# Blockwise seven-product query projection, values in DRAM, and attention run three half groups later, in a float32 attention and FFN kernel

## The reference

```
h   = einsum('bct,bcd->bdt', x, cond_weights[itok])      # mixes the 32 positions of a sequence
q, k, v = h @ wq, h @ wk, h @ wv                         # 32 query heads, 8 key/value heads, head size 128
q, k = rope(q), rope(k)
att = softmax(causal(q k^T / sqrt(128)));  o = att @ v   # one k and v per group of 4 query heads
x   = x + o @ wo                                         # 4096 -> 512
y   = einsum('bct,bcd->bdt', x, cond2_weights[itok])
x   = x + quantized(fp8(y) @ fp8(w).T + bias)            # largest value of y, and of the product, sets a scale
```

## Time and profile before

| what | us |
|---|---|
| median of 3 runs | 549.95 (549.31 to 550.25) |
| the profiled execution | 550.04 |
| its span on the core | 548.2 |
| PE busy in it | 523.0 |
| DVE busy | 354.0 |
| POOL busy | 232.0 |
| ACT busy | 212.3 |

### The profile page before, as it was taken

One profiled execution on the slowest core, in us unless ns is written; L12 is line 12 of the kernel. 1 busy time (PEld: TensorE's weight loads), 2 busy tenths in 40 slices (PEclk: granted clock), 3 DMA queues, 4 the chain that ended last, 5 costly groups with the idle time before them and its releaser, 6 DMA issues.

```text
span 548.2 us, 8916 instructions
## 1 busy us (share of the span) xinstructions
PE 523.0 (95%) x3281; PEld 417.1 (76%) x3281; DVE 354.0 (65%) x536; ACT 212.3 (39%) x372; POOL 232.0 (42%) x184
## 2 busy tenths in 40 slices
PE   4999999999999999999999999999999999999990
PEld 1987888888888888888888888888888888887530
DVE  5538255666676667666766676666666756675697
ACT  2514214342534263416341634253516251612524
POOL 3426422642664266426632673267326732610002
PEclk9899999999999999999999999999999999999995
DMA  7540500020012001201020202020202000000004
GB/s 229 194 154 0 173 2 1 1 97 1 11 68 96 0 26 50 96 0 47 29 96 0 74 3 96 0 77 0 96 0 77 5 1 0 2 1 0 2 0 153
DMA packets 18046, 26.81 MB, mean 49 GB/s; under 512 B 1995, under 2 KB 6219, under 8 KB 18028
## 3 DMA queue, kind: packets, MB, share of 16 engines
q1 hardware_dynamic: 18028, 26.57, 14.2%
HBM read 24.47 MB, written 2.10 MB: 48 GB/s over the span
## 4 chain that ended last, share of the span: by engine, by line
PE 92%; DVE 5%; DMA 1%; issue 1%; SPq 0%; ACT 0%; DVEq 0%
PE bank L524 27%; PE bank L525 26%; PE bank L526 26%; PE bank L588 3%; PE bank L575 3%; PE bank L643 1%; PE bank L516 1%; PE bank L709 1%; PE bank L504 1%; PE bank L689 1%; DVE xacc L968 1%; DMA wsc<-in_L_ffn_weight_scale 1%; DVE v_all L963 1%; DVE w L763 1%; PE bank L706 1%
## 5 line engine op out<-in xcount | busy, mean ns | idle before, releaser
L784 DVE TENSOR_TENSOR q_cos<-bank,cst 128x512 f32<-128x512 f32 x80 | 55.3, 691 | 105.1 <-ACT q_swap L394 105.1
L293 POOL TENSOR_TENSOR q_rot<-q_cos,q_swap 128x512 f32<-128x512 f32 x64 | 82.5, 1289 | 89.3 <-DVE q_swap L786 89.3
L524 PE MATMUL bank<-wo_hi,o_hi 128*128 128x512 f32 x256 | 101.6, 397 | 1.3 <-issue 1.3
L524 PE MATMUL bank<-hT_hi,wq_hi 128*128 128x512 f32 x256 | 101.3, 396 | 0.0
L525 PE MATMUL bank<-wo_lo,o_hi 128*128 128x512 f32 x256 | 99.8, 390 | 0.0
L525 PE MATMUL bank<-hT_lo,wq_hi 128*128 128x512 f32 x256 | 99.8, 390 | 0.0
L526 PE MATMUL bank<-wo_hi,o_lo 128*128 128x512 f32 x256 | 99.6, 389 | 0.0
L526 PE MATMUL bank<-hT_hi,wq_lo 128*128 128x512 f32 x256 | 99.6, 389 | 0.0
L393 ACT ACTIVATE q_swap<-bank 64x512 f32<-64x512 f32 x80 | 47.6, 596 | 132.1 <-PE bank L526 132.1
L829 DVE TENSOR_TENSOR xacc<-xacc,bank 128x512 f32<-128x512 f32 x64 | 43.4, 677 | 42.6 <-PE bank L526 42.4
L272 POOL TENSOR_TENSOR wo_lo<-raw_o,wo_hi 128x512 fp32r<-128x512 f32 x32 | 43.7, 1386 | 58.7 <-ACT wo_hi L383 58.7
(11 more groups left out here) (137 smaller groups left out, 728.6 us busy)
## 6 DMA issues: line engine op xcount, KB each, us to landing
raw_q<-in_L_attn_wq SPq DMA_DIRECT2D x8, 1024.0 KB, 5.5
raw_o<-in_L_attn_wo SPq DMA_DIRECT2D x8, 1024.0 KB, 5.3
xacc<-in_x SPq DMA_DIRECT2D x4, 512.0 KB, 8.5
raw_k<-in_L_attn_wk SPq DMA_DIRECT2D x8, 256.0 KB, 2.8
out<-xacc SPq DMA_DIRECT2D x8, 256.0 KB, 2.0
raw_o<-in_L_attn_wv SPq DMA_DIRECT2D x1, 1024.0 KB, 7.3
raw_q<-in_L_attn_wv SPq DMA_DIRECT2D x1, 1024.0 KB, 6.8
q_rot<-in_L_ffn_qweight SPq DMA_DIRECT2D x1, 1024.0 KB
```

Of the source, the lines that this page charges most:

```text
L293: pool.tensor_tensor(dst, q_cos[b][:], q_swap[b][:], ALU.add).then_inc(rope_done, 1)
L524: pe.matmul(dst, l_hi, r_hi, start=(i == 0), stop=False)
L784: dve.tensor_tensor(by_t(q_cos[b][:]), by_t(q_ps[ITEM_BANK[k]][:]), cos_b, ALU.mult).then_inc(rope_cos, 1)
```

## The change

**Query projection.** The four query heads of a group are two pairs. A pair is one 512 by 256 block of wq, and the rows are two halves of 512. Seen as a 2 x 2 by 2 x 2 block product (256 channels by one head, 256 channels by 512 rows), before it is eight block products of 6 matmuls. The change makes it of seven by Strassen and Winograd's scheme: the right sides are blocks of hT or sums of them (t_hi, t_lo, made once in the opening), the left sides are blocks of wq or sums (w_sum, made by POOL with four subtractions or additions of 128x256 for each pair, before the split into seven high and low parts). The products go to banks a, b, c, d, b, c, e; ACT saves the first in SBUF (`keep_first`) and DVE combines them with seven additions (`winograd`), three of them into SBUF and four in place in PSUM, which gives two heads for both halves of the rows.

**Halves.** The sixteen stages become sixteen halves (g, h), h being the pair of heads; each does the pair and the key of row half h. Both units of scores come at the end of half (g, 1). The softmax of unit (g-1, h) runs in half (g, h), and attend and project_out of a unit three halves after its own: (g-2, 1) in half (g, 0) and (g-1, 0) in half (g, 1). The halves before (1, 1) have no attended unit. Four units are left for after the last half, together with the rounding of the FFN weights, which was in the opening before.

**Order of PE in a half:** wait for all five cosines of the half before (and, for h = 0, for both transposes of scores, `s_turned`), attend, seven products, key, project_out 0, 1 and 2, for h = 1 both scores, project_out 3.

**Output weights.** ACT and POOL split wo of group g-1 in half (g, 1), now behind the swap and the rope_add of item 4, which is the key (item 4 in the new order; it was item 0).

**Values** go through four SBUF slots to a DRAM tensor, and 256 KB come back for each unit; POOL's copies of them (L282) go. **Opening:** the condition weights are used in float32 in place of three bfloat16 parts, selection and mixing are interleaved with the first values, the smaller constants load first, and DVE makes t and its low part between the value copies.

The core of the diff (lines that are only "..." stand for what is left out, among it most removed lines):

```diff
-SOFT_STEPS = 8
-ITEM_BANK = [0, 1, 2, 0, 1]
+SOFT_STEPS = 7
+PRODUCTS = 7
+SUMS = 7
+SUM_PRODUCT = (2, 3, 4, 5, 5, 6, 7)
+ITEM_SUM = (3, 5, 6, 7)
...
+        a_ps, b_ps, c_ps, d_ps, e_ps, spare_ps = bank[0:6]
+        product_ps = [a_ps, b_ps, c_ps, d_ps, b_ps, c_ps, e_ps]
+        item_ps = [d_ps, b_ps, c_ps, e_ps, a_ps]
+        k_ps = a_ps
+        o_ps = [c_ps, d_ps, spare_ps, e_ps]
+        o2_ps = [b_ps, c_ps, d_ps, e_ps]
+        s_ps = [spare_ps, a_ps]
+        w_ps = bank[6:8]
...
+        def left_part(h, i):
+            a11, a12 = raw_q[:, h, 0:2, 0:HD], raw_q[:, h, 2:4, 0:HD]
+            a22 = raw_q[:, h, 2:4, HD:2 * HD]
+            return (a11, w_sum[:, 1], w_sum[:, 2], a12, w_sum[:, 0], a22, w_sum[:, 3])[i]
...
+            def load_values(g, r):
+                sp.dma_start(v_st[r][:], v_rows[:, r * TPU:(r + 1) * TPU, bass.ds(g * HD, HD)]).then_inc(dma_vst[r], 16)
...
+                pool.tensor_tensor(w_sum[:, 0], a21, a22, ALU.add).then_inc(w_summed, 1)
+                pool.tensor_tensor(w_sum[:, 2], a11, a21, ALU.subtract).then_inc(w_summed, 1)
+                pool.wait_ge(w_summed, 4 * n + 1)
+                pool.tensor_tensor(w_sum[:, 1], w_sum[:, 0], a11, ALU.subtract).then_inc(w_summed, 1)
+                pool.wait_ge(w_summed, 4 * n + 3)
+                pool.tensor_tensor(w_sum[:, 3], a12, w_sum[:, 1], ALU.subtract).then_inc(w_summed, 1)
...
+            def half(g, h, split_wo=None):
+                follow = (g, 1) if h == 0 else (g + 1, 0)
+                more = not (isinstance(g, int) and g == KV - 1 and h == 1)
+                if more:
+                    sum_weights(*follow)
+                rope_add(g, h, 0)
+                rope_add(g, h, 1)
+                if more:
+                    q_low(*follow, 0)
+                    q_low(*follow, 1)
+                rope_add(g, h, 2)
+                if more:
+                    q_low(*follow, 2)
+                rope_add(g, h, 3)
+                if more:
+                    q_low(*follow, 3)
+                rope_add(g, h, 4)
                 if split_wo is not None:
...
+                    for head in range(REP):
+                        wo_low(split_wo, head, wo_lo)
+                if more:
+                    for i in range(4, PRODUCTS):
+                        q_low(*follow, i)
+                    if h == 1:
+                        k_low(g + 1)
...
+                elif hi is wo7_hi:
+                    act.wait_ge(scores_mm, 2 * KV)
+                else:
+                    act.wait_ge(wo_mm, 2 * TPU * g)
+                for head in range(REP):
+                    act.activation(hi[:, head, :], raw_o[:, head, :], ACT.Copy).then_inc(wo_hi_done, 1)
...
+                if k == 4:
+                    act.wait_ge(key_mm, 2 * g + h + 1)
+                else:
+                    act.wait_ge(sum_done, SUMS * (2 * g + h) + ITEM_SUM[k])
+                if not (isinstance(g, int) and n < 2):
+                    act.wait_ge(rope_done, n - 1)
...
+                swap(g, h, 3)
+                if more:
+                    q_high(*follow, 3)
+                swap(g, h, 4)
+                if split_wo is not None:
+                    wo_high(split_wo, wo_hi)
+                if more:
+                    for i in range(4, PRODUCTS):
+                        q_high(*follow, i)
+                    if h == 1:
+                        k_high(g + 1)
...
+            def product(g, h, i):
+                pe.wait_ge(wq_lo_done, PRODUCTS * (2 * g + h) + i + 1)
+                r_hi, r_lo = right[i]
+                three_pass(product_ps[i][:], [((wq_hi[:, i, c, :], wq_lo[:, i, c, :]), (r_hi[:, c, :], r_lo[:, c, :]))
+                                              for c in range(2)]).then_inc(prod_mm, 1)
+            def pair(g, h, last):
+                n = 2 * g + h
+                if isinstance(g, int) and n == 0:
+                    pe.wait_ge(t_lo_done, 4)
+                else:
+                    pe.wait_ge(rope_cos, 5 * n)
+                    if h == 0:
+                        pe.wait_ge(s_turned, 2 * g)
+                product(g, h, 0)
+                product(g, h, 1)
+                if last is not None:
+                    u = 2 * last[0] + last[1]
+                    pe.wait_ge(o_lo_done, BPT * u + 1)
+                product(g, h, 2)
+                if last is not None:
+                    pe.wait_ge(o_lo_done, BPT * u + 2)
+                product(g, h, 3)
+                pe.wait_ge(sum_done, SUMS * n + 1)
+                product(g, h, 4)
+                pe.wait_ge(sum_done, SUMS * n + 2)
+                product(g, h, 5)
+                if last is not None:
+                    pe.wait_ge(o_lo_done, BPT * u + 4)
+                product(g, h, 6)
+            def key(g, h):
+                pe.wait_ge(wk_lo_done, g + 1)
+                pe.wait_ge(first_kept, 2 * g + h + 1)
+                three_pass(k_ps[:], [((wk_hi[:, c, :], wk_lo[:, c, :]), (hT_hi[:, c, half_rows[h]], hT_lo[:, c, half_rows[h]]))
+                                     for c in range(KC)]).then_inc(key_mm, 1)
...
+            def project_out(g, r, j, left=(o_hi, o_lo), weights=(wo_hi, wo_lo)):
+                n = TPU * (2 * g + r) + j
                 if j == 0:
                     pe.wait_ge(wo_lo_done, REP * (g + 1))
...
+                    pe.wait_ge(o_lo_done, BPT * (2 * g + r + 1))
...
+            def half(g, h, last=None, fill=()):
+                n = 2 * g + h
                 if last is not None:
+                    pe.wait_ge(rope_cos, 5 * n)
+                    if h == 0:
+                        pe.wait_ge(s_turned, 2 * g)
                     attend(*last)
...
+                pair(g, h, last)
+                key(g, h)
+                for i in fill:
                     values(i)
                 if last is not None:
                     project_out(*last, 0)
                     project_out(*last, 1)
...
                     project_out(*last, 2)
+                if h == 1:
+                    scores(g, 0)
+                    scores(g, 1)
+                if last is not None and not (isinstance(g, int) and n == 2 * KV - 1):
                     project_out(*last, 3)
...
+            half(0, 0, fill=late[0:2])
+            half(0, 1, fill=late[2:4])
+            half(1, 0)
+            half(1, 1, last=(0, 0))
+            with pe.Fori(2, KV - 1) as g:
+                half(g, 0, last=(g - 2, 1))
+                half(g, 1, last=(g - 1, 0))
+            half(KV - 1, 0, last=(KV - 3, 1))
+            half(KV - 1, 1, last=(KV - 2, 0))
...
+            def winograd(g, h, step):
+                n = 2 * g + h
+                dve.wait_ge(prod_mm, PRODUCTS * n + SUM_PRODUCT[step])
+                if step == 0:
+                    dve.wait_ge(first_kept, n + 1)
+                    op = dve.tensor_tensor(second_u[:], b_ps[:], first_p[:], ALU.add)
+                elif step == 1:
+                    dve.wait_ge(sum_done, SUMS * n + 1)
+                    op = dve.tensor_tensor(third_u[:], c_ps[:], second_u[:], ALU.add)
+                elif step == 2:
+                    op = dve.tensor_tensor(d_ps[:], d_ps[:], first_p[:], ALU.add)
+                elif step == 3:
+                    dve.wait_ge(sum_done, SUMS * n + 2)
+                    op = dve.tensor_tensor(second_u[:], b_ps[:], second_u[:], ALU.add)
+                elif step == 4:
+                    op = dve.tensor_tensor(b_ps[:], b_ps[:], third_u[:], ALU.add)
+                elif step == 5:
+                    op = dve.tensor_tensor(c_ps[:], third_u[:], c_ps[:], ALU.subtract)
+                elif step == 6:
+                    dve.wait_ge(sum_done, SUMS * n + 4)
+                    op = dve.tensor_tensor(e_ps[:], e_ps[:], second_u[:], ALU.add)
+                op.then_inc(sum_done, 1)
...
+            def half(g, h, last=None, weights=None, fill=()):
+                if weights is not None:
+                    if h == 0:
+                        turn_scores(g - 1, 0)
+                        turn_scores(g - 1, 1)
+                    for step in range(3):
+                        soft(*weights, step)
                 if last is not None:
                     for b in range(BPT):
                         o_low(*last, b)
...
+                for step in range(5):
+                    winograd(g, h, step)
+                rope(g, h, 0)
+                winograd(g, h, 5)
+                rope(g, h, 1)
+                winograd(g, h, 6)
+                rope(g, h, 2)
+                rope(g, h, 3)
+                rope(g, h, 4)
+                for i in fill:
                     v_copy(i)
                 if last is not None:
                     accumulate(*last, 0)
+                if weights is not None:
+                    soft(*weights, 3)
+                    soft(*weights, 4)
+                if last is not None:
                     accumulate(*last, 1)
...
+                if weights is not None:
+                    soft(*weights, 5)
```

(46 more changed lines are left out.)

974 lines of the change are left out of this document (525 added, 449 removed).

## The result

The changed kernel took 740.2 us (median of 4 runs, 733.7 to 745.7) against 550.1 before (549.3 to 550.4), 190 us slower. The ratio is 1.343, 95% interval 1.339 to 1.346, and leaves out the run of 745.7, which counts as slow (the median of the other three is 738.1). The forecast was 681 with a range of 642 to 706. The sign and the main cause were right; the size was 59 us short.

A forecast was written before the change was run, and what follows sets the result against it. PE alone was taken to bound the kernel before. Opening 54.5, main part 514.5, restarts 4.5, low clock 20.4 and tail 86 gave a span of 679.9; with 1.84 outside it 681.8, stated as 681 us, range 642 to 706.

The forecast's parts named there:

- The output weights' split: In half (g, 1), PE's project_out 0 waits for POOL's low parts behind the key's rope_add: 14.0 us, in seven groups.
- Rival A: Faster: PE stays full because the four heads of wo are ready when the key ends; 524 us, chance 0.03.
- the rule named beside that rival: Trainium skill: improving a kernel generally means improving its most contended engine; here PE, which loses matmuls, giving 524 us.
- Rival C: POOL and DVE do not hinder each other: 65 us a group, 652 us in all, chance 0.16.
- Rival B: Heads split at the start of the half, only POOL and DVE's shared turns remain: about 584 us, chance 0.04.
- Attend to 1.1: In a half's walk, PE's attend matmuls take 1.1 us, the duration read from the earlier kernel's chain.
- The 2.2 us waits I cost at nothing: PE's 2.2 us waits, for accumulate 0 and for the transposes of scores, were taken to lose no clock.
- The clock behind the long wait: After gaps of 11 to 14 us PE's clock halves for 5.1 us, losing 2.55; eight gaps lose 20.4.
- rival D: The clock stays at 2.4 GHz or returns at once after the gaps: 661 us, chance 0.13.
- DVE and POOL: DVE's additions cost 0.62 to 0.69 us, also into PSUM; POOL's instructions of 256 elements cost 0.75 us.
- Both cost nothing with that cover: Value stores have four slots, 10.9 us, and reloads come a half ahead: no cost; without cover, about 3 us.
- The tail: After the last group's scores: earlier tail plus nine more results, two more attends and some waits, taken as 86 us.

The follow-up runs named there:

- experiment 3: Changed kernel with ACT and POOL splitting the output weights at the start of half (g, 1), POOL ahead of rope_add 0: 644.8 us.
- Experiments 1 and 2: Attend's matmul order exchanged: the first gave the changed kernel the old order, 701.3 us; the second gave the kernel before the new order, 575.5 us.
- experiment 5: Changed kernel plus 12 unused matmuls ahead of the attend in each half (g, 0), filling the wait for s_turned, 72 in all: 719.5 us.
- experiment 1: Changed kernel with attend back in the old order, tile by tile and inside that over the four batches: 701.3 us.
- experiment 7: Changed kernel with attend's old order, the output weights split at the start of half (g, 1), and scores transposed ahead of accumulate 3: 586.4 us.
- experiment 8: Changed kernel with old attend order, early output-weights split, scores transposed before accumulate 3, accumulate 0 before item 4's cosine and sine, value stores before first weight loads: 555.9 us.

## Why the prediction was right or wrong

The parts add up: 61.5 to the first product (forecast 54.5), 585.3 to the end of the last scores (539.4), 93.7 after it (86). The errors are 7.0 + 45.9 + 7.7 = 60.6 us, the whole difference between 740.5 and 679.9.

**The output weights' split: right.** The wait was read from POOL's order alone and put at 14.0 us in seven groups; it was 13.0, and moving the split gave back 95.4 us. Rival A stood against the same order and fell with it: PE was the busiest engine and lost 96 matmuls, and the kernel became slower, so the rule named beside that rival did not hold for this change. Rival C fell by DVE's 905 ns, and by waits of 13.0 us, which are outside its 9 to 12. Rival B's case, the split at the start of the half, is experiment 3: 644.8, where the walk gave 584. B left out the same two terms as the forecast.

**The attend's price: the first failed step.** "Attend to 1.1" took the duration from the earlier trace rows for an instruction stream whose order the diff changes. It was 2.75 at full clock, 1.65 more in 16 places, 26.4 us in all: 3.3 us a group, 5.0 in the tail's three attends. The price of a group of small matmuls belongs to its order, and I priced only its count. Experiments 1 and 2 show it from both sides.

**"The 2.2 us waits I cost at nothing": the second.** The wait's length at the attend was right (2.3), but behind it the clock fell, 3.4 or 5.1 us lost each time and 23.6 in six places, shown by experiment 5, where filling the wait kept the clock full and saved 21 us. I had a row for a gap of 4.4 us and none for a shorter one, so zero was one end of a range and not its middle. The two failed steps are linked: with the attend in its old order the same waits lost 11.4 (experiment 1). The other wait at nothing, for accumulate 0, did cost no clock here, at 1.6 us; at 2.6 us in experiment 3 it cost none either, while in experiment 7 four of its 13 waits, of 1.7 to 2.0 us, brought a drop of 1.7 us. What decides between them was not tested.

**A group's ledger**, for the three groups from 277.24 on. Forecast 71.6. Attends +3.3, second low clock +3.4, larger matmul distance +0.9 (as measured in experiment 8), restarts (a term of their own in the sum) +0.3, first low clock +0.2, waits shorter by 1.0 and 0.6: 78.1 of the measured 78.7. The smaller matmul rate was not in the forecast at all. From the attend at 180.98 to the one at 576.32, five groups took 395.3 us against 5 x 71.6 = 358.0, so 37 of the 45.9 are here; the rest, in the first halves and the last group, was not taken apart.

**The clock behind the long wait: right.** 2.55 forecast, 2.5 measured on average in seven places (2.8 in the windows shown); rival D is out, on the windows.

**DVE and POOL: right.** Additions that write PSUM 0.69 to 0.70, as taken; POOL's 256 elements took 0.73 alone against 0.75, and the splits 0.95 on average with the turns, which the walk counts apart.

**The opening: the stores' cover failed.** "Both cost nothing with that cover" rested on loads landing alone in 2.8 us. The timelines of DVE, POOL and the SP queue in the changed kernel:

```profile
52.58 0.69 DVE L962 COPY v_st<-bank 128x512 f32<-128x512 f32 x1 [5.53 <-DMA values<-v_st]
```

```profile
35.79 7.01 POOL L392 TENSOR_TENSOR o_lo<-raw_q,o_hi 128x512 fp32r<-128x512 f32 x4 [17.70 <-ACT o_hi L455]
```

```profile
42.83 0.94 SPq L283 DMA_DIRECT2D raw_q<-in_L_attn_wq  x2
43.81 0.51 SPq L293 DMA_DIRECT2D raw_o<-in_L_attn_wo  x1
44.36 1.22 SPq L280 DMA_DIRECT2D values<-v_st  x2
```

The store of the value tile stands behind the first loads of the weights, and SP issues those only when POOL has finished with raw_q, at 42.80. The store was issued at 44.36, 1.5 us behind the first of them, and shares the DMA engines with 2 MB: 8.1 us in the chain, 5.5 of which DVE waits and 2.75 PE. In experiment 8, where SP issues these stores first, PE has no such wait. The prediction even named the price without cover, "about 3 us"; the mistake was to keep it out of the sum. The values' first product came later than walked too, at 18.95 (PE's timeline) instead of 16. These two are 5.7 of the 7.0.

**The tail: size, and an error in adding.** The terms listed for it are 22.1, 35.9, 24.5, 2.2, 3.2 and 0.5 to 2; they add to 88.4 to 89.9, and the sum took 86. The 3.2 us wait at (7, 0, 0) was forecast to the digit; the attends' order added 5.0, and the clock behind the wait (670 to 675 us at 0.72) 1.4.

**The range** was too narrow on the high side: its upper end took mistakes of priced terms and none for terms held at zero. Three such zeros, the order of small matmuls (26 us), the clock behind short waits (24) and the stores (3), all pointed the same way. A cost that stands at zero can only be wrong upwards.

## What to carry to other kernels

When a diff shortens the work of the engine that bounds the kernel, walk the queues of the other engines first: who makes the next operand, and what stands ahead of it. Here five orders were worth 184 us and the saved matmuls 22 at most. Price a wait on TensorE at its length plus the clock lost behind it. Here waits of 2.1 to 2.3 us in front of small matmuls in the slow order cost more clock than their length, and one of 2.6 us elsewhere cost none, so look at the granted clock behind each kind of wait. Try a few useless matmuls in the gap: together with the windows behind it they show whether it is the clock. Compare several groups before you say that a drop has changed its length. Let consecutive small matmuls change their strip of rows.

## What the runs showed that I had not expected

- Gaps of 2.1 to 2.3 us on TensorE in front of an attend brought the granted clock to 1.2 GHz in all six groups, and it lost 3.4 us in four of them and 5.1 in two; 72 useless matmuls in these gaps made the kernel 21 us faster. A gap of 2.6 us elsewhere left the clock full (experiment 3).
- The low clock behind the same gap was half as long when the small matmuls behind it were in the fast order (11.4 us lost in all instead of 23.6).
- 32 matmuls of 32 rows take 1.10 us or 2.8 us by their order alone, with the same mean duration of 283 ns each.
- The distance between large matmuls at full clock, without waits, was 0.2266 us before and 0.2294 to 0.2332 in the changed kernel. It eats a third of what seven products save (0.93 of 2.72 us a group); its cause stays open.
